# The node stage of a graph attention kernel: ScalarE's order, log-sums by chunk and head, and where beta is added

## What is computed

```python
qk = jnp.sum(q[:, dst] * rel_k, -1) / 4.0                    # per head and edge
lse = jnp.log(segment_sum(exp(qkT - m[dst]), dst)) + m       # per node and head
h = (qk - lse.T[:, dst])[..., None] * rel_v
agg = segment_sum(h, dst)                                    # per node: 128 numbers
z = relu(agg @ z_W + z_b)
z = layer_norm(z, z_g, z_beta)                               # over 16, per head
out = layernorm(x + z.reshape(N, -1))                        # over 128
```

## Time and profile before

| what | value |
|---|---|
| median of three runs | 3016.16 us (3015.1 to 3016.63) |
| the profiled execution | 3012.32 us, span 3010.5 us |
| busy in the span | TensorE 2816.9 us (94%), VectorE 2863.3 (95%), ScalarE 2306.5 (77%), GpSimd 2400.8 (80%) |
| mean granted TensorE clock | 0.975 of full speed |
| busy tenths of the last five of 40 slices | TensorE 9 7 9 4 5, VectorE 9 7 9 5 7, ScalarE 8 5 5 3 6, GpSimd 8 4 7 7 3 |

### The profile page before, as it was taken

How to read it: one execution, slowest core, us unless ns; L and a number is a source line. 1 busy time by engine, 2 the same in 40 slices (tenths; PEclk the granted TensorE clock), 3 DMA queues, 4 the chain that set the end, 5 groups by cost and what they waited for, 6 DMA issues and landing times. The chain is left out here.

```text
span 3010.5 us, 74844 instructions
## 1 busy us (share of the span) xinstructions
PE 2816.9 (94%) x18870; PEld 2493.2 (83%) x18870; DVE 2863.3 (95%) x3093; ACT 2306.5 (77%) x5301; POOL 2400.8 (80%) x2622
## 2 busy tenths in 40 slices
PE   4669999999999999999999999999999999997945
PEld 3349999999999999999999999999999999995733
DVE  7879999999999999999999999999999999997957
ACT  2448888888888888888888888888888888885536
POOL 7778888888888888888888888888888888884773
PEclk9989999999999999999999999999999999998977
DMA  4568888888888888888888888888888888887642
GB/s 89 166 176 246 255 257 254 254 256 254 254 252 256 253 254 255 254 256 253 255 256 252 255 254 256 253 254 256 253 255 254 254 252 255 255 255 218 151 120 74
DMA packets 660920, 706.02 MB, mean 235 GB/s; under 512 B 97993, under 2 KB 554430, under 8 KB 660469
## 3 DMA queue, kind: packets, MB, share of 16 engines
q1 hardware_dynamic: 568201, 489.71, 53.9%
q0 software_dynamic: 84896, 211.12, 25.4%
q10 hardware_dynamic: 7756, 4.43, 0.6%
HBM read 473.01 MB, written 231.15 MB: 234 GB/s over the span
## 5 line engine op out<-in xcount | busy, mean ns | idle before, releaser
L1325 POOL DMA_INDIRECT e_rows<-node_table,e_gcol x1564 | 1912.1, 1223 | 420.1 <-issue 416.5
L1142 PE MATMUL banks<-w_edge,e_eat 128*128 128x240 f32 x6256 | 1396.8, 366 | 0.6 <-ACT e_ysq L1254 0.5
L1142 PEld LDWEIGHTS banks<-w_edge,e_eat 128*128 128x128 f32 x6256 | 1180.5, 190 | 84.7 <-issue 1.0
L1135 PE MATMUL banks<-e_h,e_oh 128*128 128x248 f32 x3128 | 782.9, 373 | 4.2 <-DVE e_h L1430 4.1
L1425 DVE TENSOR_REDUCE e_zs<-e_z 128x96 f32<-128x1440 f32 x391 | 642.0, 1642 | 0.2
L1135 PEld LDWEIGHTS banks<-e_h,e_oh 128*128 128x128 f32 x3128 | 563.5, 190 | 47.1 <-DVE e_h L1430 6.1
L1224 ACT ACTIVATE e_agg<-banks 128x496 f32<-128x496 f32 x782 | 458.0, 586 | 111.8 <-PE banks L1135 107.8
L1413 DVE TENSOR_TENSOR e_p<-banks,e_yr 128x960 f32<-128x960 f32 x391 | 451.8, 1155 | 28.0 <-PE banks L1142 14.0
L1430 DVE TENSOR_TENSOR e_h<-e_p,e_zw 128x960 f32<-128x960 f32 x391 | 448.9, 1148 | 1.2 <-POOL e_zw L1338 1.2
L1232 ACT ACTIVATE e_eat<-banks 128x512 f32<-128x512 f32 x391 | 233.4, 597 | 281.8 <-PE banks L1155 281.6
L1394 DVE TENSOR_TENSOR e_p<-e_p,e_rows 128x960 f32<-128x960 f32 x391 | 448.7, 1148 | 0.0
(11 more groups left out here) (414 smaller groups left out, 2647.6 us busy)
## 6 DMA issues: line engine op xcount, KB each, us to landing
tile_sums<-e_agg SPq DMA_DIRECT2D x391, 496.0 KB
e_q<-q_by_rank SPq DMA_DIRECT2D x1564, 90.0 KB
e_ea<-in_edge_attr SPq DMA_DIRECT2D x390, 256.0 KB
e_rows<-node_table,e_gcol POOLq DMA_INDIRECT x1564
edge_lse<-t_lse_sb SPq DMA_DIRECT2D x14, 448.0 KB, 3.5
edge_qk<-e_qkt SPq DMA_DIRECT2D x130, 48.0 KB
node_table<-n_tb SPq DMA_DIRECT2D x24, 240.0 KB, 2.9
n_x<-in_x SPq DMA_DIRECT2D x24, 128.0 KB, 2.6
```

The costliest lines, as they stand in the source:

```text
L1135: last = nc.tensor.matmul(sums_bank(x, loop, half)[:, (j % 2) * AW:(j % 2 + 1) * AW], oh[:, x % OR, j, :], hh[:, x % HR, j, :, :].rearrang ...
L1142: last = nc.tensor.matmul(out_ps[:, j // 2, (j % 2) * 2 * HC:(j % 2 + 1) * 2 * HC], eat[:, x % 4, j * P:(j + 1) * P], t["w_edge"][:, at:at ...
L1325: g.indirect_dma_start(out=rows[:, k, j, :], out_offset=None, in_=table, in_offset=bass.IndirectOffsetOnAxis(ap=gcol[:, kb, at:at + 1].bit ...
```

## The change

Six edits, all but two in the node stage.

1. ScalarE's Relu (c-2) moves from its fifth place to the head of the count, before L1919.
2. The columns of a row of `edge_lse` lie by chunk and then head, where they lay by head and then chunk. The same memory is then also [CE x CHUNKS, 8], and a node's log-sum is one row of 8 numbers (32 bytes). The copies from PSUM (`copy_lse`) do the reordering; the stores are the same bytes.
3. `idx` becomes place x 16 + chunk, by one more VectorE instruction of 49 columns in `edges`, and the gather brings `la`, 8 numbers a node, straight away. The mask L1725, the reduction L1743 and the tensor `oc` (now in a spare room of `edges`) go. `la` has room for all 13 turns, so the gathers wait for no reader; L1768 waits for them instead.
4. Beta is added for turns 0 to 8 ahead of the count loop, for turns 9 to 12 at the head of counts 9 to 12, as before.
5. `UP` is 36 in place of 40. The sums of turns 9 to 12 are gathered after the log-sums of turns 3 to 6, a whole turn (four blocks, one for turn 12) each.
6. The gathers' semaphores are rings of four (`GR`) for the sums and for the log-sums; each turn waits for its own (`landed`), and GpSimd waits, before gathers of turn n, for those of turn n-4.

```diff
-        lse_d = dram("edge_lse", [CE, P])
+        lse_d = dram("edge_lse", [CE * CHUNKS, H])
...
-            link(v.scalar_tensor_tensor(out=nc_, in0=nc_, scalar=-float(CE), in1=t["end_pos"][:], op0=ALU.mult, op1=ALU.add))
+            link(v.scalar_tensor_tensor(out=pos_f, in0=nc_, scalar=-float(CE), in1=t["end_pos"][:], op0=ALU.mult, op1=ALU.add))
+            link(v.scalar_tensor_tensor(out=nc_, in0=pos_f, scalar=float(CHUNKS), in1=nc_, op0=ALU.mult, op1=ALU.add))
...
-    NBK, XBR, KEPT, UP = 4, 9, 36, 40
+    NBK, XBR, KEPT, UP, GR = 4, 9, 36, 36, 4
...
+    def landed(n):
+
+        return 16 * (NBK * (n // GR) + turn(n)[0])
...
+            def gather_sums(n):
+                if n >= GR:
+                    pool.wait_ge(s_sg[n % GR], landed(n - GR))
+                for b in range(turn(n)[0]):
+                    g.indirect_dma_start(out=sums_of(n)[:, b, :], out_offset=None, in_=t["sums_d"],
...
+            def gather_lse(n):
+                if n >= GR:
+                    pool.wait_ge(s_lg[n % GR], landed(n - GR))
+                for b in range(turn(n)[0]):
+                    g.indirect_dma_start(out=la[:, n, b, :], out_offset=None, in_=t["lse_d"],
...
+            for n in range(UP // NBK):
+                gather_sums(n)
             for q in range(LR):
                 pool.wait_ge(s_ls[q], 16 * len(range(q, NSUB, LR)))
             for n in range(TURNS):
...
-                if 2 <= n < 2 + BLOCKS - UP:
-                    gather_sums(UP + n - 2)
+                gather_lse(n)
+                if 3 <= n < 3 + TURNS - UP // NBK:
+                    gather_sums(UP // NBK + n - 3)
...
+            def add_beta(n):
+                nb, rows = turn(n)
+                dve.wait_ge(s_xl[n % XBR], 16 * (n // XBR + 1))
+                v.tensor_tensor(out=xb[n % XBR][0:rows, 0:nb, :], in0=xb[n % XBR][0:rows, 0:nb, :],
+                                in1=beta_b[0:rows, :].unsqueeze(1).to_broadcast([rows, nb, F]), op=ALU.add).then_inc(s["xb"], 1)
+
+            for n in range(XBR):
+                add_beta(n)
             for c in range(TURNS + 6):
...
-                    v.tensor_tensor(out=hc(lt[rr, 0:nb, :]), in0=hc(lg[n % 3][rr, 0:nb, :]),
-                                    in1=oc[rr, bs, :].unsqueeze(2).to_broadcast([rows, nb, H, CHUNKS]), op=ALU.mult).then_inc(s["lt"], 1)
+                    if n >= XBR:
+                        add_beta(n)
...
-                    v.tensor_reduce(out=la[n % 2][rr, 0:nb, :], in_=hc(lt[rr, 0:nb, :]), axis=AX.X, op=ALU.add).then_inc(s["la"], 1)
...
-                    dve.wait_ge(s["la"], n + 1)
+                    dve.wait_ge(s_lg[n % GR], landed(n))
...
-                    dve.wait_ge(s_sg, 16 * (UP if n < UP // NBK else BLOCKS))
+                    dve.wait_ge(s_sg[n % GR], landed(n))
...
-                sc_.activation(lse_sb[:, k % LR, 0:4, :].rearrange("p t c -> p (t c)"), bank[4][:, 0:4 * P], ACT.Copy).then_inc(s_lc, 1)
+                by_place = lambda ap: ap.rearrange("p t (c h) -> p t c h", h=H)
+                by_head = lambda ap: ap.rearrange("p (t h c) -> p t c h", h=H, c=CHUNKS)
+                sc_.activation(by_place(lse_sb[:, k % LR, 0:4, :]), by_head(bank[4][:, 0:4 * P]), ACT.Copy).then_inc(s_lc, 1)
...
             for c in range(TURNS + 6):
+                n = c - 2
+                if turn(n):
...
+                    act.wait_ge(s["z_ps"], n + 1)
+                    if n >= 2:
+                        act.wait_ge(s["zc_ps"], n - 1)
+                    sc_.activation(zr[n % 2][:, 0:nb, rr], bank[1 + n % 2][:, 0:nb * rows].rearrange("p (b n) -> p b n", n=rows),
+                                   ACT.Relu, bias=zb_col[:, 0:1], scale=1.0).then_inc(s["relu"], 1)
                 n = c - 4
                 if turn(n):
...
```

More of the change, by code:

```diff
@@ L1473, in tail @@
     xt_t, st_t = flat[:, 0:2 * HALF], flat[:, 2 * HALF:4 * HALF]
-    firsts, ends, oc, idx, nident, same_c, same_b, cen = (t[k] for k in ("firsts", "ends", "oc", "idx", "nident", "same_c", "same_b", "cen"))
+    firsts, ends, idx, nident, same_c, same_b, cen = (t[k] for k in ("firsts", "ends", "idx", "nident", "same_c", "same_b", "cen"))
     back = firsts
@@ L1502, in tail @@
     ring = lambda n: [blocks4(room(NBK * P)) for _ in range(n)]
-    lg, o = ring(3), ring(2)
+    o = ring(2)
+    la = room(TURNS * NBK * H).rearrange("p (n b h) -> p n b h", n=TURNS, h=H)
     zr, zn, yc, agt = ring(2), ring(2), ring(2), ring(2)
-    lt, a1, ag, zq, y, yq = (blocks4(room(NBK * P)) for _ in range(6))
+    a1, ag, zq, y, yq = (blocks4(room(NBK * P)) for _ in range(5))
     small = lambda: room(NBK * H).rearrange("p (b h) -> p b h", h=H)
-    la, ld = [small() for _ in range(2)], [small() for _ in range(2)]
+    ld = [small() for _ in range(2)]
     lab, lex, lln, l0, lsr, lsf, lse = (small() for _ in range(7))
@@ L1526, in tail @@
         sem("carry_col"), sem("carry_by_head"), sem("carry_spread"), sem("carry_blocks"), sem("carry_of_nodes"))
-    s_sg = sem("sums_gathered")
-    s_lg = [sem(f"lse_gathered{i}") for i in range(3)]
+    s_sg = [sem(f"sums_gathered{i}") for i in range(GR)]
+    s_lg = [sem(f"lse_gathered{i}") for i in range(GR)]
     s_xl = [sem(f"x_loaded{i}") for i in range(XBR)]
@@ L1733, in _ @@
                         dve.wait_ge(s["lse"], n)
-                    v.scalar_tensor_tensor(out=l0[rr, 0:nb, :], in0=ld[n % 2][rr, 0:nb, :], scalar=0.0, in1=la[n % 2][rr, 0:nb, :],
+                    v.scalar_tensor_tensor(out=l0[rr, 0:nb, :], in0=ld[n % 2][rr, 0:nb, :], scalar=0.0, in1=la[rr, n, 0:nb, :],
                                            op0=ALU.max, op1=ALU.add).then_inc(s["l0"], 1)
[L1736 to L1742, removed]
-                    v.tensor_reduce(out=la[n % 2][rr, 0:nb, :], in_=hc(lt[rr, 0:nb, :]), axis=AX.X, op=ALU.add).then_inc(s["la"], 1)
                 n = c - 1
@@ L1911, in _ @@
             for c in range(TURNS + 6):
+                n = c - 2
+                if turn(n):
+                    nb, rows = turn(n)
+                    rr = slice(0, rows)
+                    act.wait_ge(s["z_ps"], n + 1)
[3 more added lines that the diff above has]
+                                   ACT.Relu, bias=zb_col[:, 0:1], scale=1.0).then_inc(s["relu"], 1)
                 n = c - 4
@@ L1939, in _ @@
                     sc_.activation(r1[n % 2][rr, 0:nb], l1[rr, 0:nb], ACT.Exp, scale=-0.5).then_inc(s["r1"], 1)
[L1940 to L1946, removed]
-                    sc_.activation(zr[n % 2][:, 0:nb, rr], bank[1 + n % 2][:, 0:nb * rows].rearrange("p (b n) -> p b n", n=rows),
-                                   ACT.Relu, bias=zb_col[:, 0:1], scale=1.0).then_inc(s["relu"], 1)
                 n = c - 6
```

44 lines of the change are left out of this document (15 added, 29 removed).

## The result

The changed kernel takes **3034.45 us** (median of four runs, 3032.44 to 3037.12), the kernel before in the same runs 3015.63. The ratio is 1.0067 (95% interval 1.0055 to 1.0079): slower, by some 19 to 20 us. The forecast was 3029.5 in a range of 3016 to 3039, with 0.76 on slower. The profiled execution has a span of 3035.3, and at 3037.12 it was the slowest of the four; against the span of before, which belongs to a quick one (3012.32), it is 24.8 longer.

What follows compares the result with a forecast made beforehand. Bounds: VectorE's 7.56 us a turn and an 8.17 us ring over three engines. Turn 6 +2.2, turns 6 to 13 +10.0, later turns 0.8 and edge stage 0.2 gave +13 us: 3029.5, range 3016 to 3039.

Steps and rivals of the forecast that it cites:

- A ring over three engines: Last stage: ScalarE, TensorE and VectorE wait for one another, 8.17 us between starts of L1799 (the marks of turns).
- VectorE's own 7.56: Last stage: VectorE's own work per turn before the change, 7.56 us, the second limit beside the 8.17 of the ring.
- What the change removes: VectorE's turn loses 1.80 us in turns 0 to 8, 1.20 after; none of it lies in the ring.
- The Relu's move: ScalarE's turn now first waits for the fold matmul: 1.38 us more in the ring, 9.55 at 1.2 GHz, 7.34 at 2.4.
- the matmul 1.13: TensorE's fold matmul, taken as 1.13 us within the 2.40 from ScalarE's copy L1999 to L1919.
- Six turns of seven at 1.2 GHz: TensorE's clock between turns 6 and 13: six turns of 9.55 and one of 7.34, 64.6 us against 54.6.
- The gathers: GpSimd, at 1.39 us a gather and 2.8 to land, is the bound up to turn 6, which comes 2.2 us later.
- Added ahead: Nine beta additions before turn 0, 0.60 us each, start VectorE some 2 us later than its log-sums allow, but hidden.
- The drain: Turns 13 to 18: between nothing and 1.38 plus 1.78 us more, taken as 0.8.
- TensorE at 2.4 GHz: Rival: TensorE stays fast, seven turns of 7.34 us, 3015, up to 3019 if two are slow; chance 0.16.
- VectorE as the bound: Rival: ScalarE's wait is covered and VectorE's 5.76 to 6.36 us sets the turn, 9.7 us faster, 3006; chance 0.07.
- The all-slow case: Rival: all seven turns slow, fold matmul at 2.07 us, slow gathers and full drain: +27 us, 3043; chance 0.08.

Runs made afterwards that it cites:

- the kernel before with the clock held up: The kernel before plus six 64-column matmuls, read by nobody, behind each fold matmul to hold TensorE's clock up: 3012.8 us, ratio 0.9991.
- the version with the Relu back: The changed kernel with ScalarE's Relu in its old fifth place, all else of the change kept: 3015.1 us, ratio 0.9999.
- with the clock held up: Where 7.40 is given: the changed kernel plus eleven 64-column matmuls, read by nobody, behind each fold matmul: 3018.7 us, ratio 1.0011.
- The version with the sums gathered singly and the Relu at the head: The changed kernel with the old gather order, 40 sums ahead, then one block after the log-sums of turns 2 to 10: 3036.3 us, ratio 1.0076.
- another version: The changed kernel with the Relu's old place and the old gather order (3009.1 us), plus six unread matmuls behind each fold matmul: 3003.9 us, ratio 0.9958.

## Why the prediction was right, and where it was off

**What bounds the kernel.** Right. A ring over three engines and VectorE's own 7.56 lie close together; the kernel before with the clock held up shows the second alone (7.54 to 7.63), and the version with the Relu back shows 8.16 and 8.17 in turns whose centring group took 3.75 (once 8.53), and 6.47 in the one where it took 1.97.

**What the change removes.** Right: 1.8 us a turn on VectorE bring nothing to a ring that does not pass through them. With the Relu and the order of gathers as before, the rest of the change brings 6.3 us. No run separates the two removed instructions from the smaller gathers in that; putting the additions of beta back into the turns gives up 1.2 to 1.7 of it, not clear of noise.

**The Relu's move.** The mechanism was right, the size was low. Forecast: 9.55 in a slow turn and 7.34 in a fast one. Measured: 9.55 and, with the clock held up, 7.40. The term that was too small is "the matmul 1.13". I took the fold matmul at the higher clock, since most of those in the kernel before were, and put its slow form (2.07) into a rival with 0.08. Of the seven between marks 6 and 13 five took 2.07 or 2.08. The two turns with a fast one are 9.55; those with a slow one are three times 10.50, which is 9.55 + 0.95, and once each 10.85 and 10.11. After the longer pause (3.13 us, as worked out, in place of 1.75) TensorE ran at 1.2 GHz not only for the centring group but often beyond the transposes: the fold matmul was slow in five of seven turns in all three profiles with the Relu at the head and no filling, in one of seven in the kernel before and in two of seven with the Relu back. The Trainium skill ("TensorE: Matmul & The Clock Gate", Part 1) calls the throttled state the default; the trace agrees. "Six turns of seven at 1.2 GHz" was seven of seven. With both put right the forecast is 7 x 9.55 + 5 x 0.95 = 71.6, and 71.56 was measured; the forecast had 64.6. That it fits to the digit is luck, as 10.85 and 10.11 stand 0.35 over and 0.39 under 10.50.

**The gathers.** Right that GpSimd is the bound up to turn 6: VectorE's L1775 at 2936.43 waited 4.81 us for them and stands 1.37 before the mark, as worked out, and the fold matmuls of turns 4 and 5 took 1.13. From the first log-sum gather (2879.92) to the fourth of turn 6 (2934.03) one took 1.39, as forecast, and it landed in 2.4 in place of 2.8. But the first stood 6.1 us behind the start of the stage and not 4.8, so turn 6 came 3.0 late against 2.2. The changed order as such costs less: two bounds stood close together at turn 6, 2934.6 by GpSimd and 2931.4 by the ring in the forecast. The version with the sums gathered singly and the Relu at the head is held by the ring instead, and its turn 6 comes 2 us earlier in the profile; by the runs there is no gain.

**Added ahead.** Right that it is hidden: the first log-sum difference L1775 is at 2888.68, 0.81 earlier than before, after waits for eight loads of x. The reordered copies cost nothing:

```profile
L1891 ACT ACTIVATE t_lse_sb<-banks 128x512 f32<-128x512 f32 x14 | 8.4, 597 | 11.4 <-PE banks L2036 11.4
...
L1892 ACT ACTIVATE t_lse_sb<-banks 128x384 f32<-128x384 f32 x14 | 6.8, 486 | 0.0
```

They have 597 and 485 ns before the change, 14 of each.

**The drain.** 2.4 against 0.8: the turn from mark 13 took 7.47 in place of 5.01. Most of it is one centring group at the lower clock, 1.78; the last block's fold matmul took 0.76 in place of 0.47. I had counted both terms and taken about a quarter of their bound of 3.2. The group before and after:

```profile
2987.83 1.97 PE L2096 MATMUL banks<-centring,t_x 128*128 128x256 f32 x8 [1.35 <-DVE t_x L1799]
```
```profile
3010.18 3.75 PE L2105 MATMUL banks<-centring,t_x 128*128 128x256 f32 x8 [2.73 <-DVE t_x L1806]
```

**The rivals.** TensorE at 2.4 GHz did not happen by itself; made to happen, it gave 3018.7, the upper end of what I wrote for it, with two of the seven turns slow, as I wrote there, and part of a third. VectorE as the bound was seen only with the Relu back. The all-slow case was half true: its slow fold matmuls, 5 x 0.95 = 4.8 us, are about what lies between the forecast of 3029.5 and the measured 3034.45. That they match so well is in part luck: in the profiles the change is 24.8 longer against a forecast of 13, and there the seventh slow turn (2.2), the drain (1.6) and the start of the stage (2.2, not the change's) make up most of the rest.

## What to carry to other kernels

A wait at the head of an in-order engine's turn is paid by all that is queued behind it. Before moving an instruction forward, look at what it waits for, what small instructions now run under that wait, and who waits for those; here four small instructions had covered a fold matmul for nothing. Work taken off the busiest engine pays only in turns where that engine sets the pace, so find the ring first, and price a matmul in it at the clock that it will have after the change and not before.

## What the runs showed of the hardware

- Eleven matmuls a turn whose result nobody reads took 15.7 us off the changed kernel. From turn 8 on its centring groups took 1.97, at a granted clock of 1.00, in place of 3.75 at 0.50, in all turns but one (3.64, with 0.89 and 0.69 granted). Six of them took 5 us off another version (6.6 by the ratios). At the high clock the eleven took 2.56 us. At the low one, 4.79, they delayed the work behind them by 1.25.
- A gather of 128 rows of 32 bytes landed in 2.4 us at the median, one of 512 bytes in 2.8; the Trainium skill ("DMA: Bandwidth & Descriptors", Specifications) says that under 512 B the engines do a read-modify-write, and no cost of that showed in these reads from DRAM, apart from a longest case of 5.9 against 4.7.
- ScalarE's copy of 512 columns from PSUM with a stride of 64 bytes took 0.60, as it does in order.
